# A graph network with experts: teams of two groups instead of four, and node tables stored in rank order by plain DMAs

## What is computed

```python
h = x @ W_in + b_in                                   # 128 -> 256
for l in range(3):
    agg = segment_sum(h[src], dst) / deg
    logits = concat([h, agg]) @ router_W[l] + router_b[l]   # 8 experts
    gates = softmax over the best 2, 0 for the others
    weak = relu(agg @ weak_W[l] + weak_b[l])          # 4 experts, 256 -> 256
    strong = relu(agg @ W1[l] + b1[l]) @ W2[l] + b2[l]      # 4 experts, 256 -> 512 -> 256
    moe = sum over experts of gates * expert
    h = h + sigmoid(h @ conf_W[l] + conf_b[l]) * moe
x = layernorm(x + h @ W_out + b_out)
x = layernorm(x + attention(elu(attention(x))))       # 4 heads of 32, then 1 head of 128
```

## Time and profile before

| | us |
|---|---|
| runs of the kernel before | 5935.09, 5938.35, 5938.46; median 5938.35 |
| profiled execution | 5933.33 |
| its span on the chip | 5931.7 |
| busy: POOL | 4386.1 (74%), 4519 instructions |
| busy: VectorE | 3424.5 (58%), 6554 |
| busy: TensorE | 3196.1 (54%), 11848 |
| busy: ScalarE | 1199.1 (20%), 2737 |
| preparation, to the first gather of round 0 | 337.9 |
| rounds 0, 1, 2 with the steps to the next first gather | 1105.9, 1105.7, 1221.1 |
| attention rounds, the second with the output | 1077.9, 1083.2 |

### The profile page before, as it was taken

How to read it: one execution, slowest core, us unless ns; L and a number is a source line. 1 busy time by engine, 2 the same in 40 slices (tenths; PEclk the granted TensorE clock), 3 DMA queues, 4 the chain that set the end, 5 groups by cost and what they waited for, 6 DMA issues and landing times.

```text
span 5931.7 us, 58922 instructions
## 1 busy us (share of the span) xinstructions
PE 3196.1 (54%) x11848; PEld 2024.6 (34%) x11995; DVE 3424.5 (58%) x6554; ACT 1199.1 (20%) x2737; POOL 4386.1 (74%) x4519
## 2 busy tenths in 40 slices
PE   4068889999879899988899998000000000000000
PEld 3055555557545555565556566000000000000000
DVE  5336666663556666546666665355565536566563
ACT  1022223333223233322333333000000000000000
POOL 7767777776777777767777775777777777777777
PEclk8569999998889999979999999555555555555555
DMA  3243333332433333333333331222222222222222
GB/s 85 62 144 104 105 104 104 103 102 85 140 105 104 104 104 102 101 125 103 101 103 99 104 96 45 52 56 56 56 56 56 56 52 55 55 55 55 55 55 51
DMA packets 229720, 497.87 MB, mean 84 GB/s; under 512 B 95689, under 2 KB 112130, under 8 KB 229362
## 3 DMA queue, kind: packets, MB, share of 16 engines
q0 software_dynamic: 184432, 465.31, 29.4%
q1 hardware_dynamic: 45192, 31.48, 1.8%
HBM read 463.82 MB, written 32.65 MB: 84 GB/s over the span
## 4 chain that ended last, share of the span: by engine, by line
POOL 30%; PE 25%; issue 16%; DVE 11%; DVEq 8%; DMA 6%; ACT 2%; POOLq 1%; ACTq 0%; SPq 0%
POOL ring L544 26%; PE ps_w1a L1605 5%; PE ps_w1b L1605 4%; PE ps_gate L1630 4%; PE ps_wide L1630 4%; DMA ring<-gat_tab,stage 3%; PE ps_weak_a L1617 3%; DVE ps_wide L1079 2%; PE ps_weak_b L1617 2%; DMA ring<-hidden_tab,stage 2%; POOL gat_tab L590 1%; DVE ps_wide L875 1%; DVEq L832 1%; DVE part L845 1%; DVE h_res L866 1%
## 5 line engine op out<-in xcount | busy, mean ns | idle before, releaser
L544 POOL DMA_INDIRECT ring<-hidden_tab,stage x2400 | 2302.8, 959 | 779.5 <-issue 713.4
L544 POOL DMA_INDIRECT ring<-gat_tab,stage x1600 | 1542.1, 964 | 491.8 <-issue 457.0
L834 DVE TENSOR_TENSOR ps_wide<-ps_wide,ring 128x1024 f32<-128x1024 f32 x450 | 554.7, 1233 | 312.3 <-SPq L402 186.6
L1735 PE MATMUL ps_w1a<-ident,agg_team_t 128*128 128x128 f32 x28 | 7.8, 434 | 1035.5 <-DVE agg_team_t L1157 1035.5
L1605 PE MATMUL ps_w1a<-agg_team_t,wbuf 128*128 128x512 f32 (+1 forms) x1248 | 561.7, 572 | 7.3 <-ACT strong L1287 5.9
L1630 PE MATMUL ps_gate<-wbuf,strong 128*128 128x256 f32 x2400 | 559.9, 379 | 0.0
L1605 PE MATMUL ps_w1b<-agg_team_t,wbuf 128*128 128x512 f32 (+1 forms) x1248 | 556.0, 568 | 0.0
L1630 PE MATMUL ps_wide<-wbuf,strong 128*128 128x256 f32 x2304 | 537.2, 379 | 0.0
L1630 PEld LDWEIGHTS ps_gate<-wbuf,strong 128*128 128x128 f32 x2400 | 432.6, 190 | 111.2 <-issue 47.7
L1426 ACT ACTIVATE ps_gate<-shifted 128x36 f32<-128x36 f32 x296 | 60.4, 204 | 1940.6 <-DVEq L1068 1933.0
L1630 PEld LDWEIGHTS ps_wide<-wbuf,strong 128*128 128x128 f32 x2304 | 415.3, 190 | 78.5
(11 more groups left out here) (356 smaller groups left out, 4703.9 us busy)
## 6 DMA issues: line engine op xcount, KB each, us to landing
ring<-hidden_tab,stage POOLq DMA_INDIRECT x2400, 2.8
ring<-gat_tab,stage POOLq DMA_INDIRECT x1600, 2.6
hidden_tab<-h_res SPq DMA_DIRECT2D x12, 512.0 KB, 3.8
wbuf<-in_L_gnn_strong_W SPq DMA_DIRECT2D x6, 1024.0 KB, 9.3
wbuf<-in_L_gnn_strong_W SPq DMA_DIRECT2D x12, 512.0 KB, 12.3
wbuf<-in_L_gnn_weak_W SPq DMA_DIRECT2D x6, 512.0 KB, 6.2
stage<-slot_tab SPq DMA_DIRECT2D x125, 16.0 KB
wbuf<-meta_tab SPq DMA_DIRECT2D x1, 1666.0 KB, 7.4
```

Of the source, the lines that this page charges most:

```text
L544: return pool.indirect_dma_start(out=ring[:, b, 0:width], out_offset=None, in_=table, in_offset=bass.IndirectOffsetOnAxis(ap=stage[:, half ...
L834: nc.vector.tensor_tensor(wide_s, wide_s, rows(u), ALU.add).then_inc(ring_free, 1)
```

## The change

Teams have two groups: 24 turns of two and one of a single group per hidden round. Batches of the own logits and of the tables stay at 4 groups. The order of a turn is new: VectorE adds what is left of the turn before, ranks and weighs, and then aggregates group 0 and group 1 of the next turn. TensorE does the second matmuls of strong experts 2 and 3 in the next turn. Four `strong` buffers hold the relu results; one PSUM tile `ps_w1[pair]` takes two chunks of 256 columns, so all first matmuls are 256 columns wide. The router gives its logits with the nodes on the partitions at once (9 columns move), and its bias comes as a third matmul of one row into the own logits. There is one buffer for the two aggregates, as there was one for four.

All tables but the first are in the order of the ranks: row p*49 + g. So every partition's rows lie together, and ScalarE stores them with plain DMAs (`keep_state` per turn; 13 and 7 stores for the attention tables) in place of the scatters. The first table stays in the order of the ids, but its rows have 257 floats: the last one is the place of the node in the rank tables, written by SyncE in one DMA of 6272 single numbers. Round 0 gathers rows of 1028 bytes, VectorE copies the four places of each unit to `spots` (`note_places`), SyncE stores 32 slots of places at a time in `place_tab` (`keep_places`), and rounds 1 to 4 load `place_tab` in place of `slot_tab`. In the preparation all stores of the first state stand before the wait for the records, and the wait for `s_long` stands behind the first stage load.

```diff
+BATCHES = -(-GROUPS // BATCH)
+TEAM = 2
 TEAMS = GROUPS // TEAM
-BATCHES = TEAMS + 1
+TURNS = TEAMS + 1
+PAIRS = 2
+STORES = 2 * TURNS + BATCHES
...
+        hidden_tab = [dram(f"hidden_tab{i}", [NP + 1, H if i else HP]) for i in range(LAYERS)]
...
+            for b in range(EARLY_X):
+                keep_h0(b)
+            sp.wait_ge(s_blank, 1)
+            sp.dma_start(place_tab[:, 0:COLS], slots_sb).then_inc(s_blanked, 16)
+            sp.wait_ge(s_meta, 1)
+            with nc.allow_non_contiguous_dma(reason="a column of the first table"):
+                sp.dma_start(hidden_tab[0][0:NP, H:HP].rearrange("(g p) n -> p (g n)", p=P), rank_bits).then_inc(s_place, 16)
+            for b in range(EARLY_X, BATCHES):
                 keep_h0(b)
             sp.wait_ge(s_scat, 16 * GROUPS)
             sp.dma_start(meta, meta_tab.rearrange("(p g) c -> p g c", p=P)).then_inc(s_perm, 16)
-            for b in range(EARLY_X + 2, BATCHES):
-                keep_h0(b)
...
-            sp.wait_ge(s_long, 1)
...
+                def keep_places(m, half):
+
+                    sp.wait_ge(ring_free, m * UNITS + 2 * UNITS)
+                    sp.dma_start(place_tab[:, bass.ds(m * RING, RING)], spots[:, half]).then_inc(places_kept, 16)
+
+                sp.dma_start(stage[:, 0, :], table[:, 0:RING]).then_inc(staged[0], 16)
+                if r == 1:
+                    keep_places(bodies - 1, bass.ds((bodies - 1) % 2 * RING, RING))
+                    sp.wait_ge(places_kept, bodies * 16 + 16)
                 if r == 0:
                     sp.wait_ge(s_slotst_rest, 16)
+                    sp.wait_ge(s_long, 1)
...
-                for g in range(GROUPS):
-                    ids = bass.IndirectOffsetOnAxis(ap=perm[:, g, 0:1], axis=0)
-                    if r < LAYERS - 1:
-                        pool.wait_ge(h_done, r * BATCHES + g // TEAM + 1)
-                        pool.indirect_dma_start(out=hidden_tab[r + 1], out_offset=ids, in_=h_res[:, g, :], in_offset=None)\
-                            .then_inc(table_done, 16)
-                    elif r < LAYERS + 1:
-                        pool.wait_ge(row_done, (r - LAYERS + 1) * GROUPS + g + 1)
-                        pool.indirect_dma_start(out=gat_tab[r - LAYERS + 1], out_offset=ids, in_=gat_rows[:, g, :], in_offset=None)\
-                            .then_inc(table_done, 16)
-                    else:
+                            .then_inc(ggathered[GUNITS - 1] if g < GSLOTS else x_landed[(g - GSLOTS) // (3 * BATCH)], 16)
+                if r < LAYERS - 1:
+                    pool.wait_ge(table_done, 16 * TURNS * (r + 1))
...
+            def note_places(r, u):
+
+                if r == 0:
+                    nc.vector.tensor_copy(spots[:, bass.ds((u % (2 * UNITS)) * SLOTS, SLOTS)],
+                                          ring[:, bass.ds((u % UNITS) * SLOTS, SLOTS), H].bitcast(I32))
...
                     spare = list(meanwhile)
+                    if tail:
+                        add_weak(r, q - 1, TEAM - 1, TEAM)
+                        add_strong(r, q - 1, 2, TEAM)
+                    rank_experts(r, q, size)
+                    if tail:
+                        add_strong(r, q - 1, 3, TEAM)
+                    weigh_experts(r, q, size)
                     gather_next(0)
-                    if tail:
-                        add_strong(r, q - 1, NS - 1, TEAM)
-                    rank_experts(r, q, size)
-                    weigh_experts(r, q, size)
+                    between(2 if size == 1 else 0)
                     add_weak(r, q, 0, size)
-                    for s in range(1, NS):
-                        gather_next(s)
-                        between()
-                        add_strong(r, q, s - 1, size)
-                        between()
-                        if s < size:
-                            dve.drain()
-                            add_weak(r, q, s, size)
+                    add_strong(r, q, 0, size)
+                    between(2 if size == 1 else 0)
+                    gather_next(1)
+                    if after == 1:
+                        fill_up(r)
+                    add_strong(r, q, 1, size)
+                    between(1)
...
+            def keep_state(r, q, size):
+
+                act.wait_ge(h_done, q + (r * TURNS + 1))
+                act.dma_start(hidden_tab[r + 1][0:NP, :].rearrange("(p g) n -> p g n", p=P)[:, bass.ds(q * TEAM, size), :],
+                              h_res[:, bass.ds(q * TEAM, size), :]).then_inc(table_done, 16)
...
+                those = slice(b * BATCH, min((b + 1) * BATCH, GROUPS))
+                act.dma_start(gat_tab[0][0:NP, :].rearrange("(p g) n -> p g n", p=P)[:, those, :], gat_rows[:, those, :]).then_inc(table_done, 16)
...
+                    o = ps_mo[q % 2][:, j * 16:j * 16 + NE + 1]
+                    mm(o, ones_row[:], rt_bias[0:1, r, :], start=True, stop=False)
                     for k in range(2):
-                        last = mm(ps_mo[q % 2][:, j * 16:j * 16 + NE + 1], (h_team_t, agg_team_t)[q % 2][:, k, j * P:(j + 1) * P], rt_w[:, r, k, :],
-                                  start=k == 0, stop=k == 1)
+                        last = mm(o, (h_team_t, agg_team_t)[q % 2][:, k, j * P:(j + 1) * P], rt_w[:, r, k, :], start=False, stop=k == 1)
...
+                w(pe, weak_copied, n * (2 * TEAM))
+                pe.wait_ge(tr_copied, n + 1)
                 for j in range(size):
-                    last = mm(ps_weak[1][:, j * 16:j * 16 + NE + 1], logit_t[:, j * P:(j + 1) * P], ident[0:NE + 1, 0:NE + 1], start=True, stop=True)
+                    for k in range(2):
+                        last = mm(ps_weak[1][:, j * 16:j * 16 + NE + 1], agg_team_t[:, k, j * P:(j + 1) * P], rt_w[:, r, 2 + k, :], start=k == 0, stop=k == 1)
                 last.then_inc(logits_ready, 1)
...
+                for pair in range(PAIRS):
+                    w(pe, relu_ready, n * (NS * PAIRS) + (s * PAIRS + pair - 1))
+                    for half in range(2):
+                        c = 2 * pair + half
+                        for k in range(2):
+                            last = mm(ps_w1[pair][:, half * TEAM * P:half * TEAM * P + size * P], w1_w[:, k, s, c * P:(c + 1) * P], agg_team_t[:, k, 0:size * P],
+                                      start=k == 0, stop=k == 1)
...
                     projects = tail and r == LAYERS - 1
+                    relus = (q + r * TURNS) * (NS * PAIRS) + NS * PAIRS
                     if tail:
-                        second(r, q - 1, TEAM, NS - 1)
+                        second(r, q - 1, TEAM, 2)
                     turn_agg(r, q, size)
+                    if tail:
+                        second(r, q - 1, TEAM, 3)
                     router(r, q, size)
                     strong_first(r, q, size, 0)
-                    turn_logits(r, q, size)
+                    strong_first(r, q, size, 1)
                     weak_experts(r, q, size, 0)
-                    for s in range(1, NS):
-                        if s == NS - 1 and projects:
-                            pe.wait_ge(houtT_copied, q * 2)
-                        strong_first(r, q, size, s)
-                        second(r, q, size, s - 1)
-                        if s == 2 and projects:
-                            turn_state(q, q - 1, TEAM, 12)
-                        if s == NS - 1 and projects:
-                            pe.wait_ge(relu_ready, q * 16 + (r * BATCHES * 16 + 16))
-                            project(q - 1, TEAM)
-                        if s < size:
-                            weak_experts(r, q, size, s)
+                    second(r, q, size, 0)
+                    strong_first(r, q, size, 2)
+                    second(r, q, size, 1)
+                    strong_first(r, q, size, 3)
                     if projects:
-                        pe.wait_ge(z_ready, q)
+                        turn_state(q - 1, TEAM, relus - 1)
+                    if size > 1:
+                        weak_experts(r, q, size, 1)
+                    if projects:
+                        project(q - 1, TEAM, relus)
```

391 lines of the change are left out of this document (211 added, 180 removed).

## The result

The changed kernel takes 5982.35 us (median of 4 runs, 5977.96 to 5984.29) where the kernel before takes 5936.72 (4 runs, 5934.85 to 5938.46): ratio 1.0076, 95% interval 1.0058 to 1.0093. It is **46 us slower**; 5861 was forecast. The profiled execution has a span of 5980.4 us, 48.7 more than before.

What follows compares the result with a forecast made beforehand. Each turn was taken to be bound by the longest of TensorE's, VectorE's and POOL's chains. Stages 328 + 1133 + 1082 + 1187 + 1041 + 1083 gave a 5854 us span, about 5861 measured, range 5770 to 5940.

Steps and rivals of the forecast that it cites:

- The attention round: First attention round: no scatters before it, so its first gather comes at 4811.6 instead of 4848.48, -37 us.
- round 2's stores: End of round 2: ScalarE's plain stores replace most scatters before the next first gather, 1187 against 1221.1, -34 us.
- the weights of narrow matmuls: TensorE's 256-column matmuls: weight loads doubled per column but hidden, nothing charged; a rival with loads paid had chance 0.02.
- TensorE's turn and VectorE's chain: Turn of two groups: TensorE 37.9 us; VectorE 27.8 + 0.3925 us per slot, including 12.0 before the sums.
- the end of a round: Last single group to next first gather: 26 us from first transpose to last store, plus 4.5 after h_done.
- the difference between rounds 0 and 1: VectorE's copies of places in round 0: 0.32 us per unit, turns of 43.1 us; rounds of 1133 and 1082.
- the preparation: Before round 0: own rows gathered earlier, -6.3 us, and first stage load moved ahead, -3.5; first gather at 328.1.
- the start of a round: Own logits with 24 matmuls per batch instead of 16 add 20 us, filling TensorE's 20.3 us wait; turn 0 stays at 68.
- the turns: Hidden rounds: each turn is the largest of TensorE's, VectorE's and POOL's chains, 41.0 us average in round 1.
- what the shorter tail gives: Round 1: a tail of two groups instead of four gives 1082 us, -24.
- Longer turns (slower): Rival: doubled VectorE-TensorE handovers over 72 turns; 1.1 us per turn uses up the gain, 2 us gives 6005; chance 0.14.
- Wider rows: Rival, no change: round 0's 1028-byte gathers cost +72 us, or attention rounds start no sooner, +70; chance 0.07.

Runs made afterwards that it cites:

- tables_only: Kernel before with rank-order tables, ScalarE's stores and places alone, teams of four: ratios 0.9646, 0.9670 (tables_only_2, slower chip), 0.9866 at 5854.44 us (tables_only_3).
- no_places: Changed kernel without VectorE's copies and SyncE's stores of places, all rounds loading the first table's numbers: 5914.47 us, ratio 0.9968; 0.9894 and 0.9899 on slower chips.
- bias_dve: Changed kernel with router bias added once per round by VectorE, no one-row matmuls: 0.9696, 0.9727 on slower chips; 5902.27 us, 0.9947 (bias_dve_3).
- bias_first: bias_dve plus, in every turn, one group summed before ranking and ScalarE's exponential one expert later: ratios 0.9835 and 0.9786, slower chips only.
- bias_ahead: bias_dve plus, in turn 0 only, group 2 summed ahead of the ranking: 5906.87 us, ratio 0.9957; 0.9713 on a slower chip.

## Why the prediction was wrong, step by step

**Right.** The attention round (-38.8 between the two passes, forecast -37); round 2's stores (tables_only: 33.5 us less from its first gather to VectorE's pass over the table, forecast 34); the weights of narrow matmuls; TensorE's turn and VectorE's chain; the end of a round (26.9 after the last transposes where 26 + 4.5 stood); and the difference between rounds 0 and 1, forecast 1133 - 1082 = 51, measured 58, shown by no_places to be the places (61). That it is VectorE's copies and not SyncE's stores is read from the trace: in round 0 of the changed kernel two whole units start 1.96 us apart (718.17 and 720.13) or 1.84 (733.26 and 735.10), where 1.57 stood without a copy, 0.27 to 0.39 per unit where 0.32 was summed, and tables_only has the same stores and loses some 3 us (1106.9 against 1103.7 in its round 1).

**Right by luck, the preparation.** It became 6.5 us shorter where 6.3 + 3.5 were summed, but not by the first of these. SyncE's store of the slots and its first stage load, before and after:

```profile
314.35 0.36 SPq L386 DMA_DIRECT2D slot_tab<-wbuf  x1
335.36 0.35 SPq L408 DMA_DIRECT2D stage<-slot_tab  x1
```

```profile
313.90 0.36 SPq L401 DMA_DIRECT2D slot_tab<-wbuf  x1
317.75 0.34 SPq L429 DMA_DIRECT2D stage<-slot_tab  x1
```

The own rows are gathered 7.0 us sooner (250.46 instead of 257.51), but the slots are ready only 0.45 us sooner. The gain comes from the stage load, now 17.6 us earlier; POOL's first gather starts 13.7 us behind it.

**Wrong, the start of a round.** "It fills the 20.3 us in which TensorE waited ... so that turn 0 starts 68 us into the round as before." Measured 90.6, 87.0 and 87.6 in the three rounds. The step that failed is the term of the own logits. +20 us stood for eight more instructions per batch, priced like the sixteen of 3.42 us, 0.21 each; they cost 33 us, 0.34 each (90.2 us against 57.1 in bias_dve). And full clock was granted for the first 11 us of the own logits before, for the first 5 after the change; bias_dve, whose own logits are the same instructions as before, takes 57.1 us for them where 51.7 stood, 5 us more. Both together, 38 us, exceed the 20 of cover by 18, and a "price of 0 to +12 is kept for the range" was too narrow. These 19 to 23 us per round are this step, shown by bias_dve, which gets them back; with the stalls behind them it is 74 us over three rounds.

**Wrong, the turns.** "The turn is the largest of the three each time ... gives 41.0 on average in round 1." Measured (1102.7 - 87.0) / 24 = 42.3, and 42.1 in bias_dve, where the start is right: 26 us more in round 1. The lengths of single turns say where. The turns in which the teams 20 to 22 are summed, of 28, 31 and 35 slots, take 38.6, 40.2 and 41.9 there, where VectorE's formula gives 38.8, 40.0 and 41.5. Those of the teams 4 to 6, of 37, 42 and 44 slots, take 43.6 + 48.3 + 56.7 = 148.6, and VectorE's formula gives 131.7. In that stretch POOL of bias_dve_3 (its us, busy, gathers):

```profile
1677.70:1826.30 148.60, 111.44 (x117) 0.90 0.40 108
```

117 gathers at 1.25 us are 146 of the 148.6: POOL hardly stops, and VectorE waits 14.7 us there for gathers that have not landed. POOL can be only one ring, 32 slots, ahead, so long turns in a row are paid at POOL's rate, and the short ones before and after lend it at most that. The prediction's 41.0 does not have this, though its own rule does: with the slots of the 24 teams (19 to 44, from the inputs) and POOL's 1.25 us per slot in each turn's largest of three, the three turns give 46.3 + 52.5 + 55.0 = 153.8 and the 24 turns 42.8 on average; with TensorE and VectorE alone they give 40.7. So the number that was used treats POOL nearly as if its mean, 40.7 per turn, were all that counts, and the measured 42.1 to 42.3 lies nearer to the rule than to the number. Teams of four meet the same groups in the same way (two turns of 97 and 99 us in round 1 where the shortest take 77), so teams of two could gain nothing there.

**Wrong, what the shorter tail gives.** -24 us for round 1 was to come from the shorter tail. The tail itself, from the last transposes to the next round, is 26.9 us instead of 29.8; the rest needed turns that are done sooner. bias_dve, with everything as I had supposed it at the start, has -3.7 (1102.0 against 1105.7). The table of turns shows why: it leads by 17 us at group 8, by 9 at group 24 and by 1 at group 48. From group 24 to group 48 two groups take (1075.9 - 591.9) / 12 = 40.3 us before and (1075.1 - 583.4) / 12 = 41.0 in bias_dve. Before, the turns of few slots are TensorE's, 77 us or 38.5 per two groups; with teams of two the ranking and the gates stand in front of the sums in every turn, where they stood once per four groups and behind a sum. The waits of bias_dve in these twelve turns (2078 to 2570; us, times, longest):

```profile
DVE logit L944 <- ACT logit L1338: 26.0, 12, 3.8
DVE gate_n L961 <- ACT ex L1343: 22.8, 12, 2.0
PE ps_w1a L1656 <- DVE x_res L905: 31.9, 10, 5.6
```

VectorE stands 4.1 us per turn for the logits and the exponential, and TensorE 2.7 for VectorE's sums. That the order of VectorE makes the difference is argued from these waits and the lengths of turns and isn't shown; bias_first was to show it and gave no reading on a chip of the first kind.

**The rival.** "Longer turns (slower)" named 1.1 us per turn over 72 turns as the point from which it decides, with a chance of 0.14. What came is mixed: about 1 us per turn, and a start that no rival held. The rival "Wider rows" falls with no_places. The stall of POOL at the start (45 us), which was not written down, is a sign of the late start: bias_dve shortens it to 24.2 (25 was expected), and the 5 us that bias_ahead takes off it gain nothing. What the remaining 20 cost isn't shown.

In numbers, for the 126 us between forecast and measured span: the starts 19.0 + 22.6 + 19.6 = 61; the turns 32 + 35 + 7 = 74 (rounds 1, 0 and 2, as in the line before; of the 32 the late start explains some 5, as the turns of bias_dve are that much shorter in round 1, while in round 0 they are 3 longer); the ends of rounds -3.6, -3.2 and, for round 2, -5; the preparation +3; the attention rounds -1.

## What to carry to other kernels

Before a stage is made finer, ask what its coarse form ran ahead on: here TensorE's 20 us of slack at a round's start and VectorE's sums ahead of the ranking, both used up by the change. Sum a pipeline with a bounded buffer over runs of heavy items, not by the mean of each engine, for a full ring can't lend time from one turn to the next. And where a change has halves, cost and time each alone: the tables alone gave 5854 us, and their copies were nearly free only because the turn of four groups was TensorE's. Last, where a sum is built on "the largest of the three in each turn", work out that mean as well and compare: here the rule gave 42.8 and the number used was 41.0.

## What the runs showed of the hardware that was not expected

**Small matmuls at half clock.** The own logits run back to back, and still the granted clock falls. TensorE before, at the start of round 1, in the two parts of its own logits (window, its us, busy as the trace draws it, clock, DMA share, GB/s):

```profile
1439.50:1450.50 11.00, 11.00 (x100) 1.00 0.21 62
1451.40:1491.20 39.80, 39.80 (x191) 0.50 0.43 130
```

It issues the same stream in both windows, transposes of 128 columns and matmuls of 9, and has 2.4 GHz in the first and 1.2 GHz in the second; ahead of the stream stand the matmuls of 128 and 256 columns of the last turn. Sixteen matmuls of 9 columns take 1.85 us in the first window and 3.42 in the second. In the changed kernel the full level lasts for the first 5 us of the own logits and the lower one for the other 85. It ends in turn 0: the first eight matmuls of 256 columns take 3.65 us (from 1609.49), the next eight, from 1612.98 on, 1.89.

**Pauses between instructions.** On the chips where every kernel takes 1.4 times as long, single instructions of the engines other than TensorE are as long as elsewhere and the gaps are not: tables_only_2 and tables_only_3 are the same kernel with spans of 8174.1 and 5854.5 us, and VectorE is busy for 3482.5 and 3449.0 of them, ScalarE for 1190.1 and 1200.0, POOL for 4156.6 and 4190.5 (TensorE for 3503.7 and 3219.6, at a mean granted clock of 0.692 and 0.764). VectorE in tables_only_2, the first three of four additions of one unit that follow each other without a wait, and the same line in tables_only_3, where the four are drawn as one row:

```profile
2548.33 0.49 DVE L888 SCALAR_TENSOR_TENSOR ps_wide<-ring,before_cut,ps_wide 128x256 f32<-128x256 f32 x1 [4.51 <-issue]
2550.43 0.49 DVE L888 SCALAR_TENSOR_TENSOR ps_wide<-ring,before_cut,ps_wide 128x256 f32<-128x256 f32 x1 [1.62 <-issue]
2552.53 0.49 DVE L888 SCALAR_TENSOR_TENSOR ps_wide<-ring,before_cut,ps_wide 128x256 f32<-128x256 f32 x1 [1.61 <-issue]
```

```profile
711.04 1.67 DVE L888 SCALAR_TENSOR_TENSOR ps_wide<-ring,before_cut,ps_wide 128x256 f32<-128x256 f32 x4 [0.42 <-issue]
```

0.49 us each in the one, with starts 2.1 us apart; in the other four take 1.67 us, so their starts are 0.39 apart. What makes the pauses wasn't found. They also change verdicts: bias_dve is 3% faster than the kernel before there and 0.5% here, so a ratio taken on one kind of chip doesn't hold on the other.
